# One compare for eight one-hots in the degree pass of a two-layer graph network

## The reference

```python
# block 0: two graph convolutions, with self-loops of weight 1
deg  = segment_sum(ew, dst)                     # the degree pass
dinv = where(deg > 0, rsqrt(deg), 0)
norm = dinv[src] * ew * dinv[dst]
out  = segment_sum((x @ W)[src] * norm, dst) + b   # relu after the first, sigmoid after the second
x    = layernorm(x + h)
# block 1: attention over the edges
z, rh = x @ fc_w.T, edge_attr @ fc_r_w.T
e     = leaky_relu(z[src] @ a0 + z[dst] @ a1 + rh @ a2)
alpha = softmax of e over the edges of one dst
x     = layernorm(x + relu(segment_sum(alpha * (z[src] + rh), dst) + z @ loop_w))
```

## Time and profile before

| | us |
|---|---|
| median of 3 runs | 3144.19 |
| span of the profiled execution | 4158.1 |
| GpSimd busy | 2254.0 (54%) |
| TensorE busy, matmuls | 1810.8 (44%) |
| VectorE busy | 1599.5 (38%) |

### The profile page before, as it was taken

How to read it: one execution, slowest core, us unless ns; L and a number is a source line. 1 busy time by engine, 2 the same in 40 slices (tenths; PEclk the granted TensorE clock), 3 DMA queues, 4 the chain that set the end, 5 groups by cost and what they waited for, 6 DMA issues and landing times. The chain is left out here.

```text
span 4158.1 us, 32695 instructions
## 1 busy us (share of the span) xinstructions
PE 1810.8 (44%) x10379; PEld 1679.2 (40%) x10379; DVE 1599.5 (38%) x7455; ACT 169.0 (4%) x291; POOL 2254.0 (54%) x2357
## 2 busy tenths in 40 slices
PE   1344544333347211443443446003555655555576
PEld 1234444323337111443333446002555555555576
DVE  3555323345447100244444458314222333233343
ACT  0000000000000000000000001000000000000000
POOL 7434666666660776666666650773555555555500
PEclk9756565655557555555555657555666666666677
DMA  3103323334344121112121110222323323332311
GB/s 105 30 24 85 79 61 93 105 111 119 106 119 122 52 53 40 49 53 52 51 53 50 52 42 12 52 55 67 81 72 81 83 75 80 76 84 75 79 57 36
DMA packets 325061, 287.99 MB, mean 69 GB/s; under 512 B 43178, under 2 KB 284769, under 8 KB 324866
## 3 DMA queue, kind: packets, MB, share of 16 engines
q0 software_dynamic: 75072, 155.50, 15.1%
q1 hardware_dynamic: 236886, 123.92, 10.4%
q10 hardware_dynamic: 12924, 6.41, 0.5%
HBM read 272.66 MB, written 13.40 MB: 69 GB/s over the span
## 5 line engine op out<-in xcount | busy, mean ns | idle before, releaser
L499 PE MATMUL ps<-SR,ring 128*128 128x128 f32 (+16 forms) x5844 | 1319.5, 367 | 1582.7 <-DVE SR L900 707.1
L372 POOL DMA_INDIRECT ring<-x_d,srcC x1404 | 1347.3, 960 | 1114.9 <-issue 402.4
L499 PEld LDWEIGHTS ps<-SR,ring 128*128 128x128 f32 x5844 | 1184.4, 283 | 1634.6 <-issue 1615.1
L372 POOL DMA_INDIRECT ring<-h_d,srcC x782 | 751.6, 961 | 484.3 <-issue 230.4
L900 DVE TENSOR_SCALAR SR<-iota,rankC,ewC 128x128 f32<-128x128 f32 x1404 | 395.4, 354 | 413.0 <-issue 247.3
L502 PE MATMUL ps<-SR 128*128 128x128 f32 (+12 forms) x1948 | 508.5, 348 | 80.2 <-issue 79.6
L502 PEld LDWEIGHTS ps<-SR 128*128 128x128 f32 x1948 | 428.1, 268 | 96.2 <-issue 96.0
L1001 DVE SCALAR_TENSOR_TENSOR U<-iota,rankC,U 128x128 f32<-128x128 f32 x782 | 235.0, 346 | 183.0 <-issue 182.5
L924 DVE SCALAR_TENSOR_TENSOR SR<-SR,v2B 128x128 f32<-128x128 f32 x782 | 183.7, 285 | 90.9 <-issue 90.8
L900 DVE TENSOR_SCALAR SR<-iota,rankC,cols 128x128 f32<-128x128 f32 x782 | 211.1, 346 | 2.0 <-issue 0.2
L372 POOL DMA_INDIRECT ring<-in_x_dram,srcC x160 | 153.2, 958 | 97.0 <-issue 48.2
(11 more groups left out here) (166 smaller groups left out, 1039.3 us busy)
## 6 DMA issues: line engine op xcount, KB each, us to landing
SR<-in_edge_attr_dram SPq DMA_DIRECT2D x194, 512.0 KB
ring<-x_d,srcC POOLq DMA_INDIRECT x1404
ring<-h_d,srcC POOLq DMA_INDIRECT x782
U<-lo_d SPq DMA_DIRECT2D x20, 256.0 KB
x_d<-rows SPq DMA_DIRECT2D x12, 264.0 KB
x_d<-rows SPq DMA_DIRECT2D x7, 448.0 KB, 5.2
rows<-in_x_dram SPq DMA_DIRECT2D x6, 512.0 KB
h_d<-rows ACTq DMA_DIRECT2D x12, 256.0 KB
```

Of the source, the lines that this page charges most:

```text
L372: pool.indirect_dma_start(ring[:, gg % R, k, 0:width], None, (x if p == 0 and q < R0 else table)[:, :], bass.IndirectOffsetOnAxis(ap=srcC[ ...
L499: last = nc.tensor.matmul(ps[(p * NK + k) % 2][:, lo:hi], ring[:, gg % R, j, 0:D], S[:, gg % NS, j, w0:w0 + hi - lo], start=False, stop=t ...
```

## The change

The eight tensor_scalar of a group, each with the bf16 counter iota_h and one column of rankC, become one tensor_tensor over the group's eight tiles. Its inputs are the fp32 counter iota, repeated for each tile, and the group's columns of rankC, each repeated 128 times. It writes the same bf16 one-hots to the same slot of SH. The last group's has six tiles. iota_h and the cast that made it go. The semaphores and their counts stay.

```diff
-        iota_h = sb("iota_h", [P, P], BF16)
...
             link(v.tensor_copy(pidx[:, :], pidx_i[:, :]))
-            v.tensor_copy(iota_h[:, :], iota_i[:, :])
             link(v.tensor_copy(iota[:, :], iota_i[:, :]))
...
+            def spread(n):
+                return iota[:, :].unsqueeze(1).broadcast_to([P, n, W])
+
+            def rank_of(q, n):
+                return rankC[:, q * GT:q * GT + n].unsqueeze(2).broadcast_to([P, n, W])
+
             for q in range(G):
                 if q >= ND:
                     dve.wait_ge(s("deg_summed"), q - ND + 1)
-                for j, t in enumerate(tiles(q)):
-                    last = v.tensor_scalar(SH[:, q % ND, j, :], iota_h[:, :], rankC[:, t:t + 1], None, ALU.is_equal)
-                last.then_inc(s("deg_onehot"), 1)
+                n = len(tiles(q))
+                v.tensor_tensor(SH[:, q % ND, 0:n, :], spread(n), rank_of(q, n), ALU.is_equal).then_inc(s("deg_onehot"), 1)
                 if q == 0:
                     weights()
```

## The result

The changed kernel takes 3193.67 us, the median of 4 runs (3189.51 to 3196.61), beside 3145.36 us for the kernel before (4 runs). The ratio is 1.0154, with a 95% interval of 1.014 to 1.0168: 48 us slower.

The account below looks back on a forecast made before the run. GpSimd's 2346 gathers were taken to bound the kernel: 3144 us, plus 51 us for gathers delayed by wide compares, minus 0 for VectorE's saving inside slack, gives 3195 us; range 3138 to 3256 us.

Parts of the forecast that it names:

- GpSimd bounds the timed runs (2346 x 1.26 us): All passes: GpSimd's indirect gathers, one per 1.26 us, fill 2956 us, 94% of 3144, so it hardly ever waits.
- 24 us of slack for the degree pass: Degree pass before the change: x1 stored at about 183 us, GpSimd's 161st gather needs it at 207 us.
- A compare lasts 1.22 us, one per 1.15 us: VectorE in the degree pass: 98 wide compares take 112 us instead of 127.5; the saving lies in slack, 0 us.
- One gather per two compares, 2.30 us: Degree pass: a gather waits out nearly a whole compare, so one per 2.30 us instead of 1.26; chance 0.47.
- 51 us: Degree pass: 49 gathers instead of 89 during 112 us of compares; the 40 missing cost 51 us.
- What holds a gather, and who waits: Gathers beside VectorE: one starting under an instruction with two SBUF inputs waits for its end; VectorE is never held.
- Shut out: Rival, degree pass: no gather passes between two overlapping compares, GpSimd loses about 106 us, 3250 us; chance 0.20.
- No effect: Rival, degree pass: gathers fall into step with compares or slip through often, 3144 us (3138 to 3160); chance 0.18.
- The "issue" steps as a cost of the recording: VectorE and TensorE beside gathers: steps of about 1.40 us and the span's extra 1014 us exist only when profiled.
- faster: Rival, degree pass: "issue" waits are real when timed; x1's first gather comes 85 us earlier, 3059 us; chance 0.15.
- expected shorter span: Sign in the changed kernel's profile: 98 instructions suffer less from "issue" waits than 782, so span under 4158 us.
- TensorE: Degree pass: a group's eight matmuls take 1.01 us and may give back VectorE's saving, within the slack, 0 us.

Follow-up runs that it names:

- late60: The kernel before with 104 waited-for memsets of 512 elements on VectorE ahead of the degree pass's one-hots; 3187.14 us, ratio 1.0143.
- late15: The kernel before with 26 waited-for memsets of 512 elements on VectorE ahead of the degree pass's one-hots; 3142.32 us, ratio 1.0002.

## Why the prediction was right, and where it was not

The time was forecast at 3195 us and measured at 3193.67, and the mechanism that carries the forecast was seen. One step of it was wrong all the same, and the number came out only because the timed set was of the short kind. That part was luck: in the long set the same change makes the kernel faster. Step by step:

- **GpSimd bounds the timed runs (2346 x 1.26 us).** Right in the short sets. In the profile after, it waits only 34 us for others between passes; late60 turns its two stops (45 us) into 45 us of lost time.
- **24 us of slack for the degree pass.** Right: late60 gives 23, late15 shows 17 us of delay at no cost.
- **A compare lasts 1.22 us, one per 1.15 us.** 1.21 and 1.13. The pass ends at 146.5 us, forecast 148.
- **One gather per two compares, 2.30 us.** 2.27 us, and 72 gathers out at 148 us (forecast 70; 112 in the profile of late15, in which GpSimd is not disturbed).
- **51 us.** Pass 1 starts its first gather at 1064.1 us, and at 1016.9 in late15 (rows below), so 47 us later, and 48 in the medians. Between 29 and 146 us 54 gathers go out where late15 has 94; 40 x 1.25 = 50 us. The forecast's own product, 40 x 1.26, is 50 and not 51, and it took 112 us for the 98 compares, which are 111. The first x1 gather itself moved further, from 209.1 to 268.2 us, 59 us: the look-ups of pass 0, which also hold gathers, now run before it and not behind it. That part is no loss: the 160 gathers before it are 59 us longer than in late15 (213.9 us busy for 154.7), but the 1404 from x1_d and x2_d are 9 us shorter (1361.3 for 1370.1).
- **What holds a gather, and who waits.** Too simple on both sides. Not only two SBUF inputs hold one: at 16.02 us, in the trace that the prediction read, a gather takes 1.19 us, and the only VectorE work beside it is a copy and a cast with one input each, the cast from 16.27 to 17.09 us. And VectorE can be held too: with compares of four tiles it loses 0.05 us per gather.
- **Shut out.** Refuted: in the changed kernel itself gathers get in after every second of the compares, which follow without a gap, and with two-tile compares after every fourth one. What held the gather of 350.83 us for two instructions stays open.
- **No effect.** Its mechanism exists: with a compare every 1.40 us each gather meets one only. It was not this kernel's case since 1.13 us is shorter than the 1.24 us that a gather needs to come back. The inference quoted from the Trainium skill ("SBUF — State Buffer", who interferes with whom), that tensor_tensor does not disturb descriptor generation, does not hold for these indirect gathers: 1.97 us under compares with both inputs in SBUF, 0.94 us with one of them in PSUM.
- **The "issue" steps as a cost of the recording.** Wrong, and this is the one step of the prediction that failed. It explained away the difference between a span of 4158 us and a median of 3144. The 1014 us lie between two kinds of sets and not between profiled and timed runs. The count itself (what GpSimd needs if nobody is late) was right for the short sets, and they are what was timed. The *faster* rival, which took the steps for real, gave 85 us; in the long set it is 74 us, and its place, x1's first gather at about 260 us, was measured at 258.85. So the forecast holds for one kind of set and the rival for the other. The expected shorter span of the changed kernel's profile came (3189.9 us) but for another reason, its kind of set; in the long one it went from 4158 to 4076 us.
- **TensorE.** It kept up with VectorE in the short set. Its eight matmuls took 0.61 us in most of the pass; at 101.44 us, for instance, the granted clock was 1.00, the upper level of 2.4 GHz (its mean is 0.86 from 29 to 65 us and 0.95 from 73 to 146). The 1.01 us of the earlier trace rows are from a stretch (300 to 304 us) with a granted clock of 0.50, the lower level of 1.2 GHz, behind ten microseconds of which TensorE had been busy for 7.4.

The first gather of pass 1 in the order of time, in the changed kernel and in late15:

```profile
1064.10 0.94 POOL L371 DMA_INDIRECT ring<-h_d,srcC  x1 [13.50 <-DMA h_d<-rows]
```

```profile
1016.94 0.94 POOL L372 DMA_INDIRECT ring<-h_d,srcC  x1 [13.33 <-DMA h_d<-rows]
```

And late15's gathers between 29 and 146 us, beside the 54 of the changed kernel:

```profile
L372 POOL DMA_INDIRECT ring<-in_x_dram,srcC x94 | 89.7, 954 | 28.6 <-issue 28.6
```

## What to carry to other kernels

Before VectorE is given fewer and longer instructions beside GpSimd's indirect DMAs, ask which of the two engines the span waits for, and whether the long instruction reads two operands from SBUF. A gather that starts under it waits for its end, so the loss goes in steps: a gather comes with the next instruction end at or after the 1.24 us that it needs to come round, every 1.34 us for ends every 0.34 us, every 1.40 for ends every 1.40, every 2.27 for ends every 1.13. A near miss is made up by VectorE: with ends every 0.60 us the second one is 0.04 us early, and gathers came every 1.25 us, at the cost of 0.05 us of VectorE each. So shorter is not always better. By that stretch two compares of four tiles in place of one of eight would cost the gathers next to nothing (an estimate), while four of two tiles cost 8 us. The four-tile kernel was not timed in a short set. One operand in an idle PSUM bank took the whole loss away. And when a span and a median differ by a third, profile the same kernel again before deciding which of the two the waits belong to.

## What the runs showed that I had not expected

The same program takes 3141 to 3146 us in some sets and 4158 to 4166 in others. In the long ones, VectorE's and TensorE's instructions start on a grid of 0.7 and 1.4 us while gathers run (in the first trace 11 us after gathers had begun again at 172.95 us), and are free again 14 us after the gathers have stopped at 127.2. In the changed kernel's long run, at one gather per 2.27 us, VectorE shows no steps at all during the pass. In the long run of the kernel with gaps they are there, at one gather per 1.40 us. With the counter in PSUM, gathers come at 1.25 us again and the steps are back (compares 22 us apart; TensorE starts one matmul every 2.80 us, and a group has eight):

```profile
80.01 1.23 DVE L874 TENSOR_TENSOR SR<-ps,rankC 128x1024 bf16<-128x1024 f32 x1 [21.18 <-remote]
```

So in a long set the steps seem to go with the rate of gathers. TensorE has two instructions per matmul there and lags; a wide compare is then late by waiting for it, 16 groups on. All long sets with a chip on record are of one chip and all short ones of others, which speaks for the chip, but only three chips are on record, and what it is about the chip was not found.
